# Where TensorE forms a pair's in-tile products in a Mamba-2 layer, and where VectorE forms y

## The reference, cut to what matters

```python
proj = h @ in_proj_w                      # gate (4096), x/B/C (4096+128+128), dt (64)
hbc  = silu(causal_conv4(x/B/C) + conv_b) # four taps along the tokens
cum  = cumsum(dt * A)                     # per head, within a chunk
Y_diag = ((C B^T) * decay * dt) @ x       # inside a chunk
Y_off  = exp(cum) * (C @ state)           # from the state carried between chunks
y      = Y_diag + Y_off + D * x
hidden = y * silu(gate)
out    = rmsnorm(hidden) @ out_proj_w
```

## Time and profile before

| | |
|---|---|
| median of 3 runs | 1984.53 us (1983.23 to 1986.12) |
| the profiled execution: its time | 1986.35 us |
| the profiled execution: its span | 1984.4 us |
| PE busy | 1921.5 us (97%) |
| DVE busy | 1524.9 us (77%) |
| ACT busy | 1306.4 us (66%) |
| POOL busy | 830.2 us (42%) |

### The profile page before, as it was taken

One profiled execution on the slowest core, in us unless ns is written; L12 is line 12 of the kernel. 1 busy time (PEld: TensorE's weight loads), 2 busy tenths in 40 slices (PEclk: granted clock), 3 DMA queues, 4 the chain that ended last, 5 costly groups with the idle time before them and its releaser, 6 DMA issues.

```text
span 1984.4 us, 42840 instructions
## 1 busy us (share of the span) xinstructions
PE 1921.5 (97%) x12436; PEld 1578.5 (80%) x12436; DVE 1524.9 (77%) x2858; ACT 1306.4 (66%) x2978; POOL 830.2 (42%) x997
## 2 busy tenths in 40 slices
PE   6999999999999999999999999999999999999998
PEld 5888578888888857888878886788888887688886
DVE  6885578888788458888868845888887883588886
ACT  4662389999555138888845513888885551488885
POOL 2210168888200016777710001677770000177776
PEclk9999999999999999999999999999999999999999
DMA  6330246656422014444432201444442210244442
GB/s 229 119 119 1 93 154 202 209 192 207 132 74 85 22 45 144 153 146 153 140 102 74 84 32 37 155 149 148 155 148 91 85 63 22 72 153 148 152 153 77
DMA packets 119601, 234.06 MB, mean 118 GB/s; under 512 B 10560, under 2 KB 48640, under 8 KB 119040
## 3 DMA queue, kind: packets, MB, share of 16 engines
q1 hardware_dynamic: 119552, 233.41, 35.8%
HBM read 194.05 MB, written 36.18 MB: 116 GB/s over the span
## 4 chain that ended last, share of the span: by engine, by line
PE 64%; issue 22%; ACT 9%; DVE 2%; POOL 1%; ACTq 1%; DMA 1%; POOLq 0%; DVEq 0%; SPq 0%
PE bank L665 25%; PE bank L914 9%; PE bank L901 5%; PE bank L890 4%; PE bank L881 3%; PE bank L803 2%; PE bank L873 2%; PE bank L795 2%; PE bank L764 2%; PE both L795 2%; ACT span_b L1183 2%; PE both L665 2%; ACT place L1183 2%; ACT shared L1189 1%; PE bank L817 1%
## 5 line engine op out<-in xcount | busy, mean ns | idle before, releaser
L665 PE MATMUL bank<-xn_r,w_r 128*128 128x512 f32 x2268 | 617.7, 412 | 8.6 <-issue 3.1
L665 PEld LDWEIGHTS bank<-xn_r,w_r 128*128 128x128 f32 x2268 | 415.1, 190 | 114.9 <-issue 34.8
L1354 DVE SCALAR_TENSOR_TENSOR conv_acc<-bank,conv_sb,conv_acc 128x511 f32<-128x511 f32 (+2 forms) x408 | 304.3, 746 | 52.5 <-ACT conv_acc L1096 18.9
L542 POOL TENSOR_TENSOR rstd<-var_eps,minus_half 128x4 f32<-128x4 f32 (+2 forms) x12 | 9.7, 808 | 645.8 <-DVE var_eps L1283 645.8
L914 PE MATMUL bank<-wo_n,place 128*128 128x256 f32 x1024 | 255.2, 392 | 1.6 <-DVE place L1505 1.6
L1270 DVE TENSOR_TENSOR place_r<-bank,place_r 128x512 fp32r<-128x512 f32 (+1 forms) x320 | 186.8, 632 | 81.2 <-ACT place_r L1032 81.2
L1032 ACT ACTIVATE place_r<-bank 128x512 fp32r<-128x512 f32 (+1 forms) x320 | 159.1, 556 | 129.6 <-PE bank L665 104.4
L563 POOL TENSOR_TENSOR shared<-shared,c_t 128x768 f32<-128x768 f32 x128 | 234.4, 1832 | 0.0
L914 PEld LDWEIGHTS bank<-wo_n,place 128*128 128x128 f32 x1024 | 184.1, 189 | 43.2 <-issue 21.3
L585 POOL TENSOR_TENSOR sumsq<-sumsq,place 128x512 f32<-128x512 f32 x127 | 162.1, 1276 | 109.7 <-ACT place L1085 109.7
L665 PE MATMUL bank<-place_r 128*128 128x512 f32 (+3 forms) x960 | 189.2, 338 | 8.3 <-DVE place_r L1270 6.0
(11 more groups left out here) (159 smaller groups left out, 3499.6 us busy)
## 6 DMA issues: line engine op xcount, KB each, us to landing
place_r<-cum_rows SPq DMA_DIRECT2D x128, 512.0 KB, 3.9
w_r<-pair_split SPq DMA_DIRECT2D x96, 512.0 KB, 3.7
w_r<-qkv_split SPq DMA_DIRECT2D x48, 512.0 KB, 4.0
pair_split<-w_r SPq DMA_DIRECT2D x32, 512.0 KB, 4.1
qkv_split<-w_r SPq DMA_DIRECT2D x16, 768.0 KB, 3.9
w_r<-qkv_split SPq DMA_DIRECT2D x48, 256.0 KB, 3.2
wo_n<-out_split SPq DMA_DIRECT2D x96, 128.0 KB, 3.5
raw<-in_w_pair SPq DMA_DIRECT2D x32, 256.0 KB, 3.9
```

What stands on the lines that cost most here:

```text
L665: ins = mm(out, lhsT=w(a), rhs=m(b), start=(start and i == 0), stop=(stop and i == 2), **kw)
L1354: stt(out=conv_acc[:, back:W], in0=src[:, 0:W - back], scalar=conv_sb[:, ch, TAPS - 1 - back:TAPS - back], in1=conv_acc[:, back:W], op0=AL ...
```

## The change

On TensorE `in_block(n)` leaves its place between `make_states(n)` and `project_out(n-1)`. It is now issued in the next pair, between that pair's transposes and `off_block(n)`; for pair 31 it comes directly in front of `off_block(31)`, behind `project_v`. On VectorE, in every pair but 0 and 31, taps 1 and 2 of the next pair's convolution move in front of `base` and `gated`, and tap 3 stays behind them. No instruction is added or dropped, and no DMA is moved in any queue's list.

```diff
@@ TensorE, pair @@
                     if before > 0:
                         turn_x(b, n, par)
+                        in_block(b, n - 1, 1 - par)
                         off_block(b, n - 1, 1 - par)
...
                     make_states(b, n, par)
-                    in_block(b, n, par)
                     if before > 0:
                         project_out(b, n - 1, 1 - par, isinstance(n, int) and n == 1, False)
@@ TensorE, after the last pair @@
                     project_v(b + 1, 0, 0, 0)
+                in_block(b, NPAIR - 1, 1)
                 off_block(b, NPAIR - 1, 1)
@@ VectorE, pair @@
                         base, gated = tail(n - 1, 1 - par)
+                        if more:
+                            for back in range(1, TAPS - 1):
+                                conv_tap(K + n + 3, ch, bank[1], back)
                         base()
                         gated()
                     if more:
-                        conv_taps(K + n + 3, ch, bank[1])
-                        if not begin:
+                        if begin:
+                            conv_taps(K + n + 3, ch, bank[1])
+                        else:
+                            conv_tap(K + n + 3, ch, bank[1], TAPS - 1)
                             dve.wait_ge(s_hid_ready, N + 1)
```

## The result

The changed kernel takes 1989.97 us (median of 20 runs, 1985.65 to 1995.54), the kernel before 1984.88 on the same chips (20 runs, 1979.29 to 1987.55). The ratio is 1.003, interval 1.0021 to 1.0038: slower by 0.3%. The profiled execution has a span of 1990.2 against 1984.4.

A forecast was written before the change was run, and what follows sets the result against it. TensorE bounds the kernel now; after the change its saved 0.35 us a pair becomes a wait for `hid`. Steady pairs about 0 plus edges +4.1 on 1984.5 give 1988 us; range 1966 to 1999.

The forecast's parts named there:

- The 0.35 of TensorE: TensorE's work in a steady pair: one entry and one exit of half-width blocks gone, 0.35 us less (0.33 to 0.38).
- the seam: On TensorE between `in_block` and `off_block`: taken to cost 0.05 us, 0.20 if a full change.
- VectorE's chain: Taps, y and `gated` in a steady pair: `hid` done 4.46 us after the first transposes, 4.62 in slow pairs.
- Rival 2: VectorE, start of y: held until tap 2 has ended, `hid` 0.22 us later a pair, 2012 us; chance 0.10.
- Rival 1: `hid` in time for `project_out`, so TensorE does not wait: 0.26 to 0.35 us less a pair, 1956 us; chance 0.18.
- Rival 3: TensorE's seam or new neighbours cost as much as the old changes: pairs stay 7.8 us, 1988 us; chance 0.06.
- the steady pairs of sequences 1 and 2: 54 pairs there: slow-form waits add between 0 and 8.6 us in all; taken as +2.2.
- The slow form of `gated`: VectorE, y to `gated`: 0.16 to 0.2 us above 0.79 in 28 pairs, where the wait is a register's.
- The edges: First and last pairs of each sequence, where TensorE waited already: +4.1 us together.
- The ends: Pairs 30 and 31: +1.3 us a sequence in the first three, +0.6 in the last, +4.5 together.
- The starts: Pairs 0 to 2: about -0.4 us in sequences 1 and 2, +0.5 in sequence 0, together -0.4.
- The late end of the states: Pair 30: states end 0.86 us later, at 4.53 after the transposes, delaying copy and `conv_end`; +0.5 to +0.6 in every sequence.

The follow-up runs named there:

- run 3: The changed kernel with y and `hid` behind the first tap, so taps 2 and 3 follow `hid`: 1952.38 us, ratio 0.9835 to the kernel before.
- run 4: The changed kernel without y's own instruction (term D x left out, `hid` is bank 5 times the gate): 1948.52 us, ratio 0.9814 to the kernel before.
- run 5: The changed kernel with the wait for y last of three in `gated` and that for `hid` last in `project_out`: 2004.68 us, ratio 1.0103.
- run 9: The changed kernel with long-met waits moved from `gated` to y, and the fetched-weights wait in front of `make_states`: 1980.79 us, ratio 0.9982.
- run 2: The kernel before with only VectorE's half of the change, `in_block(n)` still behind `make_states(n)`: 2110.11 us, ratio 1.0632.
- run 6: The changed kernel with `in_block(30)` and `in_block(31)` back behind their own states: 1991.88 us, ratio 1.004 to the kernel before.

## Why the prediction was right, point by point

- **The 0.35 of TensorE** is there, as 0.32. The chain of run 3 is 7.50, not 7.47; the 0.32 between it and the earlier trace rows is what one entry and one exit are worth. That the seam is free is shown by the loads of the changed kernel, where the trace has no idle between L901 and L890. The Trainium skill, TensorEngine Tiling (Array Packing), Key Properties, says that a change of the tiling mode drains TensorE and a change of the tile alone does not; the trace agrees (0.17 at entry and exit, nothing at the seam).
- **VectorE's chain** came out within 0.05 at each step, against the first transposes in sequence 2: tap 1 at 1.46 (forecast 1.42), tap 2 at 2.36 (2.31), y at 3.02 (2.98), `hid` done at 4.49 (4.46), the load at 4.63 (4.60). In sequence 0 the pair came out at 7.76 for 7.81, -0.05 where -0.09 was forecast.
- **Rival 2, y held until tap 2 has ended, is refuted.** y starts 0.66 behind tap 2's start, 0.09 before the 0.75 of the tap are over. The Trainium skill, VectorE: DVE Perf Modes, says under The DRAIN you can't avoid that an instruction waits for an empty pipe, and in the same paragraph that one which is not held starts earlier; the trace agrees with the second sentence, which I had left out in weighing the first.
- **Rival 1, `hid` in time, gives what it said**, when its condition is made true: 1956 was worked out, 1952.4 (run 3) and 1948.5 (run 4) were measured. Its condition, y behind `off_block` and not behind tap 2, was named there. It does not hold in this change, and moving one tap makes it hold.
- **Rival 3, the change doesn't do what it says**, is refuted by the rows of the seam, and by run 3.
- **Step that was mis-sized: the steady pairs of sequences 1 and 2**, +2.2 ("half of them had it before, +4.3; I take half of that"). They measured +5.6. The slow form of `gated` did not depend on the edit: the register step of 0.04 is in exactly the 28 pairs that had it, and it counts now, since `hid` has no slack any more. The old share of slow pairs was no reason to take half of its cost. 26 of the 28 lie in the steady pairs, which is 26 x 0.15 = 3.9. The rest is 0.04 in all 54, whose load starts at 4.63 and not at 4.60 (2.0), less 0.2 in the first steady pairs, which are still at 7.75. Runs 5 and 9 show both: with the waits placed otherwise the alternation goes, in 5 by making all pairs slow and in 9 by making all fast.
- **The edges** were forecast at +4.1 and measured +2.4 in these two traces. The ends are +3.6 for 4.5: pair 30 is longer by 0.63 to 0.76 (0.5 to 0.6), and behind pair 31 `project_v` to the sums of squares by 0.46 (0.5), but the DMA landed sooner after its start. The starts are -1.3 for -0.4: all four are shorter, most in sequences 1 and 2 (0.5 each); the forecast's own terms, twice -0.4 and +0.5, make -0.3, and the +0.5 in sequence 0 did not come. The late end of the states (1313.94 - 1310.29 + 0.86, which is 4.51 and not 4.53) did what was said of it: pair 30 takes 7.40 or more in every other trace but that of run 2, the only one with TensorE's old order, and the transfer starts 0.7 to 0.9 later. What it costs against the place of `in_block(31)` is not shown: no run moved the transfer alone. The forecast has no term for the clock, which fell at the ends only with the block in its new place (see behind run 6); this execution of the change was one without a fall.

The sum hit better than its terms, and that is luck: about 0 for the steady part where +4.8 was measured, +4.1 for the edges where +2.4 was, and -1.4 between the two executions in parts that the change doesn't touch. The errors have opposite signs.

## What to carry to other kernels

When products move from in front of a dependent step to behind it, follow the value that the step waits for: here the gain of TensorE was real in every pair, and the change gave it away only because one tap, 0.9 us from start to start, stood in front of the two instructions of VectorE that had to be quick. Put the producer of the late value where its own inputs are complete (y behind `off_block`), and let the work that has slack (taps 2 and 3) go behind it. On an instruction that a bottleneck waits for, write no waits that are long met: hang them on something earlier. And where an engine waits for a transfer, leave the work that is ready in front of that wait (this from the traces alone).

Half a change says little of the whole where the parts share a buffer. Both halves alone were slower than the whole, each through a wait of a bank (1 and 5) that the other half had relieved.

## What the runs showed of the hardware

- Of several waits in front of one instruction the first written stays on it, and the others take a semaphore step ahead of it (one step for two waits in `gated`). If a register step is needed for one of the others, that step holds the first wait and everything starts behind it. The same three waits of `gated` give 0.78 from y to `hid` in the order of the change, 0.94 in it with a register step between, and 0.88 with y's last; from `hid` to the load of `project_out` it is 0.05 with no register step and 0.13 with one. By turning the order alone the steady pairs became 7.2 us longer (run 5, 15 us in the medians), and by moving the waits 10.5 us shorter (run 9, 9 us in the medians).
- With the block that was ready moved behind a wait for a DMA, the granted clock fell to its lower level behind that wait in 7 of 24 places, and in none of 12 with the block in front of it. A fall cost some 1.5 us.
- A stretch of half-width blocks costs about 0.32 us for going in and coming out: 28 products in one stretch for 12 and 16 in two saved that in each of some 110 pairs (run 3, whose span is 33.8 us shorter than the kernel before's).
